# Three attentions and one banded convolution of a MetaFormer kernel, each begun one FFN tile sooner

## What is computed

```python
x = x + L0_conv(ln_c(x))          # deformable attention, see below
t = tokens(x); t = t + ffn(ln_t(t), L0 weights); x = back(t)
x = x + L1_conv(ln_c(x))          # 7x7 + 5x3 + 3x5 + 7x1*1x7 + 5x1*1x5 depthwise, + bias
t = tokens(x); t = t + ffn(ln_t(t), L1 weights); x = back(t)

def L0_conv(x):                   # 3x3 depthwise; stride 2 for key and off
    value, query, key, off = dw(x, w_v, 1), dw(x, w_q, 1), dw(x, w_k, 2), dw(x, w_off1, 2)
    o = gelu(layernorm(off) * ln_g + ln_b)
    pos = tanh(o @ w_off2 + ref)
    v = bilinear_sample(value, pos)
    attn = query^T key * 32**-0.5              # per head of 32
    return w_out @ (attn @ v)                  # computed as query x (key^T v) x w_out

def ffn(x):                       # 4 experts, the best 2 of a softmax gate
    g = renormalised top-2 of softmax(x @ gate_w + gate_b)
    return sum_e g[e] * (gelu(x @ w1[e] + b1[e]) @ w2[e] + b2[e])
```

## Time and profile before

| | us |
|---|---|
| median of 3 runs | 1609.75 |
| lowest and highest | 1603.1, 1610.59 |
| profiled execution | 1609.45 |
| its span, first to last instruction | 1607.6 |
| TensorE busy (matmul) | 1430.1 |
| VectorE busy | 1140.9 |
| ScalarE busy | 726.1 |
| GpSimd busy | 510.7 |

### The profile page before, as it was taken

One profiled execution on the slowest core, in us unless ns is written; L12 is line 12 of the kernel. 1 busy time (PEld: TensorE's weight loads), 2 busy tenths in 40 slices (PEclk: granted clock), 3 DMA queues, 4 the chain that ended last, 5 costly groups with the idle time before them and its releaser, 6 DMA issues.

```text
span 1607.6 us, 21544 instructions
## 1 busy us (share of the span) xinstructions
PE 1430.1 (89%) x6736; PEld 1059.2 (66%) x6736; DVE 1140.9 (71%) x2881; ACT 726.1 (45%) x1508; POOL 510.7 (32%) x533
## 2 busy tenths in 40 slices
PE   4977677998779999998888999999999999998998
PEld 3654654556545677665555577787888788877786
DVE  6837867489984644359896444587787877689787
ACT  5622253246533444454644244454444544356554
POOL 4051143011360000011163000254344634465575
PEclk9997777999889999999989999999999999999999
DMA  4433034134333312341351422343224422221121
GB/s 121 99 91 109 25 107 123 47 104 118 82 86 92 92 50 57 103 119 56 100 128 52 132 66 61 76 111 109 62 80 113 108 67 60 72 79 60 53 69 56
DMA packets 168547, 136.37 MB, mean 85 GB/s; under 512 B 114928, under 2 KB 162162, under 8 KB 168050
## 3 DMA queue, kind: packets, MB, share of 16 engines
q1 hardware_dynamic: 163458, 129.74, 29.6%
q0 software_dynamic: 3072, 4.82, 1.2%
q10 hardware_dynamic: 1904, 0.43, 0.1%
HBM read 95.30 MB, written 39.13 MB: 84 GB/s over the span
## 4 chain that ended last, share of the span: by engine, by line
PE 50%; issue 13%; DVE 10%; POOL 7%; ACT 5%; DMA 1%; SPq 1%; ACTq 0%; POOLq 0%; DVEq 0%
PE at_ps L1349 10%; PE y_ps L1201 7%; PE h_ps L1208 5%; PE h_ps L1210 5%; PE h_ps L1209 5%; POOL pix_mem L1075 4%; PE y_ps L1190 4%; PE y_ps L1191 3%; PE y_ps L1192 3%; PE at_ps L1268 3%; DVE vq_mem L1554 2%; ACT ln_cen L868 2%; POOL ln_rstd L1048 2%; PE lb_ps L1163 2%; PE lg_ps L1176 1%
## 5 line engine op out<-in xcount | busy, mean ns | idle before, releaser
L1003 ACT ACTIVATE hidden<-h_ps,b 128x448 f32<-128x448 f32 x609 | 384.0, 633 | 618.7 <-PE h_ps L1210 606.1
L1208 PE MATMUL h_ps<-xh,w1h 96*128 96x448 f32 x672 | 366.6, 546 | 2.6 <-ACT hidden L1003 1.3
L1048 POOL TENSOR_TENSOR ln_rstd<-ln_ve,minus_half 112x4 f32<-112x4 f32 x112 | 152.5, 1361 | 659.7 <-DVE ln_ve L1493 659.5
L1201 PE MATMUL y_ps<-hidden,w 128*96 128x448 f32 x672 | 324.1, 567 | 14.3 <-ACT hidden L1003 13.7
L1510 DVE SCALAR_TENSOR_TENSOR part<-y_ps,b,gate_t 96x448 f32<-96x448 f32 x224 | 151.5, 676 | 214.3 <-PE y_ps L1201 170.1
L1067 POOL CAST in_w<-hidden 128x448 fp32r<-128x448 f32 x273 | 200.0, 736 | 242.6 <-ACT hidden L1003 161.8
L1209 PE MATMUL h_ps<-xl,w1h 96*128 96x448 f32 x672 | 249.9, 372 | 0.0
L1210 PE MATMUL h_ps<-xh,w1l 96*128 96x448 f32 x672 | 249.4, 371 | 0.0
L1208 PEld LDWEIGHTS h_ps<-xh,w1h 96*128 96x128 f32 x672 | 130.1, 194 | 90.1 <-issue 61.2
L1209 PEld LDWEIGHTS h_ps<-xl,w1h 96*128 96x128 f32 x672 | 131.5, 196 | 66.9 <-issue 61.4
L868 ACT ACTIVATE ln_cen<-ln_cen,ln_rstd 112x96 f32<-112x96 f32 x448 | 130.3, 363 | 79.0 <-POOL ln_rstd L1048 78.8
(11 more groups left out here) (186 smaller groups left out, 2153.2 us busy)
## 6 DMA issues: line engine op xcount, KB each, us to landing
gate_t<-gates_dram SPq DMA_DIRECT2D x112, 336.0 KB, 3.2
value_pairs<-pix_mem SPq DMA_DIRECT2D x56, 168.0 KB, 3.1
...
```

Of the source, the lines that this page charges most:

```text
L1003: act.activation(to[:, :], h_ps[c % H_BANKS][:, 0:TILE], ACT.Gelu, bias=b1[l][:, c:c + 1]).then_inc(gelu_done, 1)
L1048: pool.tensor_tensor(ln_rstd[n % 2][:, :], ln_ve[n % 2][:, :], minus_half[0:SUB, 0:NSUB], ALU.pow)\
L1201: pe.matmul(y_ps[e % Y_BANKS][0:C, 0:TILE], w2[l][:, c, :], hidden[c % HID_RING][:, :], start=(j == 0), stop=(j == CPE - 1)).then_inc(hid_ ...
L1208: pe.matmul(ps, hi, xh[:, ring(k)], start=True, stop=False)
```

## The change

Attentions 2 and 3 begin one tile sooner, (0,2) and (2,2), so that stage 0 of attention 2 shares tile (0,2) with stage 6 of attention 1. The fills of image 1 begin in tile 3 of slot 3 instead of tile 4, and its weights and accumulator loads come one tile sooner too. To make room, "a" jobs of images 2 and 3 and "c" jobs of image 1 are placed anew (three tiles more in slot 0's first tiles, three fewer in slot 3's), attention 1's query taps end in stage 5, and image 2's last tile is no longer handed over directly. In the lead, one job moves from place 0 to place 1 of step 7; key diagonals, one group of query taps, the key convolutions, GELU and tanh of attention 0, the spreading of w_out and the folding of the taps change their places; and the first gates are read in lead step 13 and ranked in step 14. Only order and waits change; no operation is added or removed. Context is left out of the diff:

```diff
@@ -49,7 +49,8 @@
-FILL_STEP, FILL_CHUNK, FILL_PITCH, FILL_MM = 4, 2, 7, 3
+FILL_STEP = {1: 4, 3: 3, 4: 4, 5: 4}
+FILL_CHUNK, FILL_PITCH, FILL_MM = 2, 7, 3
@@ -66,15 +67,18 @@
-ATTN_SLOT = {2: 0, 3: 2}
+ATTN_START = {2: (0, 2), 3: (2, 2)}
...
-              (-1, 7): [("a1", 4)], (-1, 8): [("a1", 5), ("a1", 6)], (-1, 9): [("a2", 0), ("a2", 1)],
+              (-1, 7): [None, ("a1", 4)], (-1, 8): [("a1", 5), ("a1", 6)], (-1, 9): [("a2", 0), ("a2", 1)],
...
-              (-1, 13): [("f0", 3), ("f0", 4)], (-1, 14): [("f0", 5), ("f0", 6)], (0, 0): [("a2", 4)], (0, 1): [("a2", 5)],
-              (0, 2): [None, ("a2", 6)]}
+              (-1, 13): [("f0", 3), ("f0", 4)], (-1, 14): [("f0", 5), ("f0", 6)], (0, 0): [("a2", 4), ("a2", 5)],
+              (0, 1): [("a2", 6), ("a3", 0)], (0, 2): [("a3", 1), ("a3", 2)],
+              (1, 6): [("f2", 6), ("a3", 3)], (2, 0): [("a3", 4), ("a3", 5)], (2, 1): [("c1", 0), ("a3", 6)],
+              (2, 2): [("c1", 1), ("c1", 2)], (2, 6): [("f3", 6), ("c1", 3)], (3, 0): [("c1", 4), ("c1", 5)],
+              (3, 1): [("c1", 6)], (3, 2): []}
@@ -109,9 +113,9 @@
-DIRECT = (0, 2, 3)
+DIRECT = (0, 3)
...
-GATE_STEP = {(-1, LEAD - 1): (0, 0), (0, 0): (0, 1),
+GATE_STEP = {(-1, LEAD - 2): (0, 0), (0, 0): (0, 1),
@@ -129,18 +133,19 @@
-        return [(1, p + 4)]
-    for b, first in ATTN_SLOT.items():
-        if slot == first and p >= 3:
-            return [(b, p - 3)]
-        if slot == first + 1 and p < 3:
-            return [(b, p + 4)]
-    return []
+        stages = [(1, p + 4)]
+    else:
+        stages = []
+    for b, (first, step) in ATTN_START.items():
+        stage = (slot - first) * TILES + p - step
+        if 0 <= stage < TILES:
+            stages.append((b, stage))
+    return stages
...
-        i = ((slot - first) * TILES + p - FILL_STEP) * CHUNKS + c - FILL_CHUNK
+        i = ((slot - first) * TILES + p - FILL_STEP[first]) * CHUNKS + c - FILL_CHUNK
@@ -444,7 +449,7 @@
-        GEN_STEP = {(1, 3): 0, (3, 3): 1}
+        GEN_STEP = {(1, 3): 0, (3, 2): 1}
@@ -452,18 +457,18 @@
-        Q_ROUNDS = {4: (0, 5), 5: (5, 8), 6: (8, 9)}
+        Q_ROUNDS = ({4: (0, 5), 5: (5, 8), 6: (8, 9)}, {4: (0, 5), 5: (5, 9)})
...
-        QUERY_CONV = {(0, 9): (0, 0), (0, 10): (0, 1), (1, 3): (0, 2), (3, 2): (1, 0), (3, 8): (1, 1), (4, 2): (1, 2)}
-        QUERY_TAKE = {(0, 11): (0, 0), (1, 2): (0, 1), (1, 5): (0, 2), (3, 8): (1, 0), (3, 11): (1, 1), (4, 5): (1, 2)}
-        KEY_CONV = {(0, 2, 10): 0, (0, 2, 11): 1, (0, 3, 0): 2, (1, 1, 4): 0, (1, 1, 5): 1, (1, 1, 7): 2}
-        KEY_TAKE = {(0, 2, 10): 0, (0, 2, 11): 1, (0, 3, 3): 2, (1, 1, 5): 0, (1, 1, 6): 1, (1, 1, 8): 2}
-        DIAG_AT = {(4, 11): ("query", 0), (5, 1): ("query", 1), (5, 4): ("query", 2), (6, 0): ("key", 0),
-                   (6, 3): ("key", 1), (6, 6): ("key", 2)}
+        QUERY_CONV = {(0, 9): (0, 0), (0, 10): (0, 1), (2, 10): (0, 2), (3, 3): (1, 0), (3, 8): (1, 1), (4, 2): (1, 2)}
+        QUERY_TAKE = {(0, 11): (0, 0), (1, 2): (0, 1), (2, 11): (0, 2), (3, 8): (1, 0), (3, 11): (1, 1), (4, 5): (1, 2)}
+        KEY_CONV = {(0, 2, 11): 0, (0, 3, 0): 1, (0, 3, 1): 2, (1, 1, 4): 0, (1, 1, 5): 1, (1, 1, 7): 2}
+        KEY_TAKE = {(0, 3, 0): 0, (0, 3, 1): 1, (0, 3, 3): 2, (1, 1, 5): 0, (1, 1, 6): 1, (1, 1, 8): 2}
+        DIAG_AT = {(4, 11): ("query", 0), (5, 1): ("query", 1), (5, 4): ("query", 2), (5, 8): ("key", 0),
+                   (5, 9): ("key", 1), (5, 10): ("key", 2)}
@@ -475,10 +480,10 @@
-                at = FILL_STEP * CHUNKS + FILL_CHUNK + FILL_PITCH * (FILLS // PARTS * (piece + 1) - 1) + 5
+                at = FILL_STEP[CONV_SLOT[b]] * CHUNKS + FILL_CHUNK + FILL_PITCH * (FILLS // PARTS * (piece + 1) - 1) + 5
...
-                ACC_LOAD[CONV_SLOT[b], 3 + piece] = b, piece
+                ACC_LOAD[CONV_SLOT[b], FILL_STEP[CONV_SLOT[b]] - 1 + piece] = b, piece
@@ -750,6 +755,9 @@
+                if 0 in stages and 6 in stages:
+                    for q in range(Q):
+                        load_quarter(stages[0], q)
...
                     store_attn(stages[6], 0)
@@ -757,7 +765,7 @@
-                if 0 in stages and slot >= 0:
+                if 0 in stages and 6 not in stages and slot >= 0:
@@ -962,11 +970,11 @@
-                    if stage == 2 and c == (10 if b == 0 else 9):
+                    if stage == 2 and c == (8 if b == 0 else 9):
                         gelu_off(b)
...
-                    if stage == 2 and c == 11:
+                    if stage == 2 and c == (10 if b == 0 else 11):
                         tanh_pos(b)
@@ -1011,7 +1019,7 @@
-                        if slot < 0 and c == (APPLY_DEEP[job.place] if deep(job) else LEAD_APPLY[job.place] if p not in (7, 11) else 10 if p == 7 else 7) or slot >= 0 and c == APPLY and job.place == 0:
+                        if slot < 0 and c == (APPLY_DEEP[job.place] if deep(job) else LEAD_APPLY[job.place] if p not in (7, 11) else 11 if p == 7 else 7) or slot >= 0 and c == APPLY and job.place == 0:
@@ -1019,7 +1027,7 @@
-                    if (slot, p) in GATE_STEP and c == (8, 11 if u in SPLIT_SLOTS else 10)[GATE_STEP[slot, p][1]]:
+                    if (slot, p) in GATE_STEP and c == (8 if slot >= 0 else 11, 11 if u in SPLIT_SLOTS else 10)[GATE_STEP[slot, p][1]]:
...
                         take_gates(*GATE_TURN[slot, p])
@@ -1398,7 +1406,7 @@
-                if (slot, p) == (-1, 3):
+                if (slot, p) == (-1, 4):
                     spread_w_out()
@@ -1558,7 +1566,7 @@
-                q0, q1 = Q_ROUNDS.get(stage, (0, 0))
+                q0, q1 = Q_ROUNDS[b == 1].get(stage, (0, 0))
@@ -1787,7 +1795,7 @@
-            TAPS_LEAD = {0: dict(none, combine2=1, end=1)}
+            TAPS_LEAD = {0: dict(none, combine2=1, end=1), 1: dict(none, combine0=5, combine1=3, combine2=4, end=3)}
@@ -1800,7 +1808,7 @@
-                        done = ((first - slot) * TILES + FILL_STEP - p) * CHUNKS + FILL_CHUNK + FILL_PITCH * f + 4.9
+                        done = ((first - slot) * TILES + FILL_STEP[first] - p) * CHUNKS + FILL_CHUNK + FILL_PITCH * f + 4.9
@@ -1811,11 +1819,10 @@
-                ops = [op for b, stage in stages for op in attn_taps(b, stage)]
+                taps = {stage: attn_taps(b, stage) for b, stage in stages}
+                ops = [op for some in taps.values() for op in some]
...
-                if by_stage.get(0) == 3:
-                    dve.wait_ge(conv_st[0], 16 * CG * PARTS)
@@ -1825,7 +1832,7 @@
-                    if ops and stage in (TAPS_SLOT if slot >= 0 else TAPS_LEAD):
+                    if taps[stage] and stage in (TAPS_SLOT if slot >= 0 else TAPS_LEAD):
@@ -1837,6 +1844,8 @@
+                        if by_stage[0] == 3:
+                            dve.wait_ge(conv_st[0], 16 * CG * PARTS)
@@ -1874,9 +1883,14 @@
-                    if owner[name] in GATE_STEP or slot < 0 and (slot, p) in GATE_STEP:
-                        gates = GATE_STEP[(slot, p) if slot < 0 else owner[name]]
-                        if name == (("normalize1", "scores")[gates[1]] if slot >= 0 else "combine1"):
+                    if (slot, p, name) == (-1, LEAD - 2, "end"):
+                        read_scores(0, 0)
+                    if (slot, p, name) == (-1, LEAD - 1, "combine0"):
+                        rank_gates(0, 0)
+                        pick_gates(0, 0)
+                    if owner[name] in GATE_STEP:
+                        gates = GATE_STEP[owner[name]]
+                        if name == ("normalize1", "scores")[gates[1]]:
...
                             rank_gates(*gates)
@@ -1902,9 +1916,9 @@
-                if (slot, p) == (-1, 3):
+                if (slot, p) == (-1, 4):
                     expand_w_out()
-                if (slot, p) == (-1, 10):
+                if (slot, p) == (-1, 8):
                     fold_taps()
```

## The result

The changed kernel takes 1630.89 us, the median of four runs (1629.49 to 1632.86); the kernel before, beside it, 1608.05. The ratio is 1.0134, with a 95% interval of 1.0109 to 1.0158. The forecast was 1614.5, with a range from 1599 to 1626, so the time lies above it. The profiled execution of the changed kernel took 1629.49 us, that of before 1609.45: +20.0, where the sum said +5.0.

What follows compares the result with a forecast made beforehand. TensorE, busy 89% of the span, was taken as the bound, so gains had to come from its idle stretches. -8.0 - 6.2 + 2.5 + 6.6 - 2.2 + 3.8 + 8.5 = +5.0 on 1609.45 gave 1614.5 us, range 1599 to 1626.

Steps and rivals of the forecast that it cites:

- part 5: Image two's stages 1 to 6 and the tile left free: sum -2.2 us, with -1.5 for tile (1,3).
- Part 7: Tile (3,3): the fill's fourth band is issued 7.7 us after the tile's start, so TensorE waits: +8.5 us.
- part 6: Image three's stages and image one's fill: stages -14.3, gates +3, one norm -0.6, a light tile +15.7; sum +3.8 us.
- Part 1: Lead up to the first gathers: a1's tile 4 stored after the value stores, first gather near 82.4 instead of 91.86; -8.0 us.
- The folding: In the lead, folding the convolution's taps two steps earlier can hold the normalisation before the last four gathers: 1.5 us back.
- Part 2: Last lead step: gates of the first FFN read a step earlier remove waits on exp and TensorE; -6.2 us.
- Parts 3 and 4: Tile (0,1): another normalised tile between gathers, +2.5 us; tile (0,2): image two's stage-0 taps inside stage 6, +6.6 us.
- rival (a): Faster, 1600.4 us: lead's gain stands whole, VectorE's waits in (0,2) take in the taps, gates' shift free; chance 0.25.
- rival (c): Slower, 1619.5 to 1622.5 us: in the lead, ScalarE's key diagonals keep the first gathers where they are; chance 0.28.
- sign of being wrong: Wrong if the first tile starts later than 206, or if (3,3) has no TensorE wait of some 8 us.

Runs made afterwards that it cites:

- e5_jobs: The kernel before with the lead's edits alone, plus image two's last three tiles normalised as in the changed kernel; 1597.42 us, ratio 0.9923.
- e3_both: The changed kernel with the tap DMAs issued in (1,0) instead of (1,1) and band 3 loaded in (3,2) instead of (3,3); 1615.02 us, ratio 1.0040.
- e1_taps: The changed kernel with the block of small tap DMAs (`load_taps`) issued in (1,0) instead of (1,1); 1621.74 us.
- e13_conv: e7_attn3 with image one's convolution a tile sooner, as in the changed kernel, and band 3 loaded in (3,2) behind band 2; 1607.82 us, ratio 0.9989.
- e7_attn3: The changed kernel with attention 2 and image one's convolution where they were before, attention 3 still begun in (2,2); 1603.48 us.
- e12_place: e5_jobs with a1's tile 4 back in place 0 of lead step 7 and its scaling one chunk sooner; 1600.19 us.
- e11_fold: e8_gelu with the folding of the convolution's taps back in lead step 10; 1594.64 us.
- e10_gates: e5_jobs with the first gates read, exponentiated and ranked in lead step 14, as before the change; 1599.43 us.
- e8_gelu: e5_jobs with GELU and the copy of the transposed gates ahead of a waiting scaling on ScalarE in the last lead step; 1593.24 us, ratio 0.9894.
- e9_taps_end: e5_jobs with attention 2 begun in (0,2), its stage-0 taps at that tile's end, and the tap DMAs a tile sooner; 1605.27 us.
- e14_jobs3: e5_jobs with the normalised tiles of images three and one placed as in the changed kernel, attentions and convolution unmoved; 1597.40 us.

## What the prediction had right and wrong

The parts measured alone add up: e5_jobs -10.6, attention 2 +7.3, attention 3 +6.1 and the convolution +4.3 give +7.1, and e3_both, which holds them all, lies 7.0 above the kernel before. The tap DMAs' and the band's places are the other 15.9. Each part is uncertain by some 2 to 4 us, so the closeness is partly luck.

- **Missed, part 5, tile (1,3), -1.5.** This is the step that failed. It was taken as a gain, because the tile no longer follows a stage 6, and it was +8.0. I listed the queues past which the moved steps go, but looked only at instructions that the diff moves. `load_taps` keeps its place while the stage around it changes, and its 16.5 us in the queue got ahead of the next tile's load (e1_taps). This term alone is 9.5 of the 15 us. With this term right the sum would have been 1624; the misses below make up the rest.
- **Part 7, right in mechanism and size, one cost missing.** Wait and issue came out as worked out (8.49 us for 8.5, 7.8 for 7.7); the lower clock after the wait, 2.9 us (29.82 against 26.90 for the same matmuls), did not stand in the sum.
- **Missed, part 6, "the fill itself is TensorE's work wherever it lies".** The work is the same, but not the clock that it meets: +4.5 from (3,2) to (4,2), 3.7 of it at the clock (e13_conv against e7_attn3). With the band mended (e3_both) the way from the end of stage 6 to (4,2) is 20.7 longer than before, where 15.7 were taken. The stages gave 14.3 where 11.9 were taken.
- **Part 1, right sum by luck, wrong reason.** The last gather is 7.8 us sooner, -8.0 was forecast. But the store's place, on which the part rested, has at most 0.9 of it (e12_place): what counts is the end of the train, and with the first gather at 79 or at 86 it comes within 0.9 us. Which of the other edits (diagonals, query taps, GELU, w_out) brings the rest wasn't tried alone. The folding, taken at 1.5, costs 2.0 of the train and 4.0 at the first tile (e11_fold).
- **Part 2, too large.** 3.3 of 6.2: a wait on ScalarE took the place of the old ones (e10_gates, e8_gelu). The lead as a whole gave 11.0 of 14.2.
- **Parts 3 and 4** said +9.1, measured +10.8 for the tile; the taps alone are 5.4 of it (6.6 forecast), and the added normalised tiles alone are +3.7 there and -2.5 in (0,1) (e14_jobs3; part 3 had +2.5). Their price is VectorE's, not the tile's (e9_taps_end): rival (a), in which they fit into waits, was wrong for that reason.
- **The chances.** Slower by over 0.5% had 0.32, and that it came is no credit to the reason given for it: rival (c) had the first gathers staying late, and the first one starts at 79.2. Neither sign of being wrong that was named came up: the first tile starts at 203.6, before 206, and (3,3) has its wait. Both looked only at the terms of the sum. The range reached 1626 because every bound was put on terms that I had named; nothing was left for a term that I hadn't.
